# Second and third attention of a vision tower: score tiles of three heads over one image's own 37 keys, values spread by image, and a later fill of the routed rows

## The reference, cut to what matters

```python
# second: causal, B x 37 x 192, H = 12, D = 16
q, k, v = jnp.split(layer_norm(x, ln1_w) @ c_attn_w.T, 3, axis=-1)
scores = jnp.einsum('bhqd,bhkd->bhqk', q, k) * (1.0 / math.sqrt(D))
scores = jnp.where(causal, scores, -jnp.inf)
y = jnp.einsum('bhqk,bhkd->bhqd', softmax(scores), v)      # then @ c_proj_w.T, + x
# third: no token sees itself, one scale per head
attn = jnp.einsum('bhid,bhjd->bhij', q, k) * scale[None, :, None, None]
attn = jnp.where(diag[None, None, :, :], -jnp.inf, attn)
out = jnp.einsum('bhij,bhjd->bhid', softmax(attn), v)      # then @ w_proj.T + b_proj, + x
```

## Time and profile before

| what | value |
|---|---|
| median of 3 runs | 2166.01 us (2151.96 to 2166.42) |
| the profiled execution's own time | 2172.53 us |
| its span, first to last instruction | 2170.6 us |
| TensorE's mean granted clock | 0.817 of 2.4 GHz |
| TensorE busy | 1868.5 us, 86% |
| first attention and tokens | 0 to about 316 us |
| second attention, first mask to last projection | 316.0 to 484.4 us |
| ffn 0 and its routing | 484.4 to 640.7 us |
| third attention, first mask to last group before the fourth's projections | 648.3 to 820.4 us |
| all later stages | 848.4 to 2170.6 us |

### The profile page before, as it was taken

How to read it: one execution, slowest core, us unless ns; L and a number is a source line. 1 busy time by engine, 2 the same in 40 slices (tenths; PEclk the granted TensorE clock), 3 DMA queues, 4 the chain that set the end, 5 groups by cost and what they waited for, 6 DMA issues and landing times.

```text
span 2170.6 us, 35211 instructions
## 1 busy us (share of the span) xinstructions
PE 1868.5 (86%) x12440; PEld 1723.5 (79%) x12440; DVE 1134.4 (52%) x3189; ACT 799.2 (37%) x1907; POOL 588.7 (27%) x1369
## 2 busy tenths in 40 slices
PE   7999999996938997998999888977998999889980
PEld 7999888876937777988898778876888898788870
DVE  2423245554327554675577643345775577643436
ACT  1211124323414333553454334434454454334420
POOL 3333241231046433123422310025313412310021
PEclk8855557657966656998998899998999999799995
DMA  4039400003420000001000046651001000046630
GB/s 117 18 107 286 138 1 15 14 24 91 163 78 23 1 15 27 1 1 56 15 2 14 27 139 199 210 170 33 4 1 55 16 1 14 13 150 203 203 107 28
DMA packets 77409, 151.00 MB, mean 70 GB/s; under 512 B 6344, under 2 KB 56626, under 8 KB 77141
## 3 DMA queue, kind: packets, MB, share of 16 engines
q1 hardware_dynamic: 70902, 136.49, 19.7%
q0 software_dynamic: 6336, 12.26, 2.0%
HBM read 108.67 MB, written 41.05 MB: 69 GB/s over the span
## 4 chain that ended last, share of the span: by engine, by line
PE 52%; issue 16%; DVE 14%; DMA 6%; POOL 4%; SPq 3%; ACT 3%; another core or an unknown queue 0%; DVEq 0%; POOLq 0%; ACTq 0%
PE ps_proj L1020 9%; PE ps_o L1075 7%; PE ps_pt L994 6%; DMA w_in<-w_all_dram 5%; PE ps_proj L1095 5%; PE ps_score L1053 4%; PE ps_proj L1033 4%; PE ps_score L1166 4%; PE ps_proj L1149 3%; PE ps_proj L947 2%; SPq L823 2%; ACT w_hi L1281 1%; PE ps_score L968 1%; DVE prob L1439 1%; DVE negmax L1438 1%
## 5 line engine op out<-in xcount | busy, mean ns | idle before, releaser
L1166 PE MATMUL ps_score<-w,hid 128*112 128x192 f32 (+2 forms) x1680 | 306.3, 335 | 14.1 <-DVE x L1717 6.2
L1166 PEld LDWEIGHTS ps_score<-w,hid 128*112 128x112 f32 (+2 forms) x1680 | 278.0, 180 | 16.8 <-issue 8.5
L1330 POOL TENSOR_SCALAR tmp<-rs,var 111x1 f32<-111x1 f32 x154 | 55.4, 360 | 855.9 <-DVE rs L1410 855.4
L1260 ACT ACTIVATE probt<-ps_pt 111x333 f32<-111x333 f32 x308 | 137.8, 447 | 338.7 <-PE ps_pt L994 336.6
L994 PE MATMUL ps_pt<-const,prob 111*111 111x111 f32 x924 | 198.8, 335 | 52.6 <-ACT probt L1260 40.6
L1271 ACT ACTIVATE hid<-ps_proj 128x224 f32<-128x224 f32 (+2 forms) x360 | 133.6, 382 | 265.9 <-PE ps_proj L1149 252.4
L994 PEld LDWEIGHTS ps_pt<-const,prob 111*111 111x111 f32 x924 | 150.0, 223 | 89.7 <-issue 54.5
L1075 PEld LDWEIGHTS ps_o<-v,probt 111*111 111x111 f32 x1584 | 213.5, 215 | 1.1 <-issue 0.5
L1075 PE MATMUL ps_o<-v,probt 111*111 111x65 f32 (+1 forms) x1584 | 208.1, 282 | 0.0
L1318 POOL DMA_INDIRECT tin<-rows_out,idx x66 | 68.0, 1030 | 499.8 <-issue 384.0
L1255 ACT ACTIVATE prob<-prob 111x333 f32<-111x333 f32 x308 | 145.8, 477 | 62.9 <-DVE prob L1439 57.6
(11 more groups left out here) (239 smaller groups left out, 4381.0 us busy)
## 6 DMA issues: line engine op xcount, KB each, us to landing
w_in<-w_all_dram SPq DMA_DIRECT2D x66, 768.0 KB, 4.4
w<-w_all_dram SPq DMA_DIRECT2D x50, 576.0 KB, 5.2
rows_in<-w_lo SPq DMA_DIRECT2D x1, 12320.0 KB, 64.5
rows_out<-w_lo SPq DMA_DIRECT2D x1, 9240.0 KB, 90.1
tin<-rows_in SPq DMA_DIRECT2D x36, 224.0 KB
rows_out<-tout SPq DMA_DIRECT2D x36, 168.0 KB
patch<-patches_dram SPq DMA_DIRECT2D x11, 333.0 KB, 3.2
wo<-wo_all_dram SPq DMA_DIRECT2D x6, 576.0 KB, 3.8
```

What stands on the lines that cost most here:

```text
L1166: last = pe.matmul(bank[0:n, 0:C], hid[:, i % 2, m, at:at + n], w2[:, slot, m, :], start=(m == 0), stop=(m == FC - 1))
L1260: act.activation(probt[:, n % 4, :, :], ps_pt[0:TG, 0:3 * TG].rearrange("p (c n) -> p c n", c=3), ACT.Copy).then_inc(pt_taken, 1)
```

## The change

Q and K of the two attentions are laid out in 2 chunks instead of 3 each, so a block has 4 QK steps instead of 6. A chunk holds, at rows 0 to 47 and 64 to 111, three heads each. When ScalarE copies Q it does so three times, each time with a scale (hscale) that is zero but for one of the three heads; so for each image a tile of 111 columns arises: three heads by 37 queries. S multiplies it (stationary) by the 37 keys of the same image: 12 products of 111 by 37 per group instead of 12 of 111 by 111, in one unit of 4 x 111 columns over both PSUM banks, with two mask products of 222 columns instead of four of 333. VectorE takes one maximum and one subtraction over 444 columns, ScalarE one exponential, TensorE four transposes instead of twelve, ScalarE one copy.

V is copied three times by ScalarE with a scale that is 1 for the tokens of one image and 0 for the others, into vimg, where each head has three images' 16 values and one of ones each. PV is 12 products with 37 stationary columns (queries) and 51 moving ones (three images by 17), into 37 partitions. The output is turned by six transposes instead of two.

`short_order` is the new list: S(n), [slot 0], PV(n-1), E(n), [slot 1], PT(n), OT(n-1), [slot 2], Y(n-1), [slot 3]. There is one W1 step less in each of the two attentions: at the end of the first attention and at the end of ffn 0. The W1 of ffn 0's first matrix moves from g = 2 to n = 7 of CAUSAL; those of the T5 layer in DIAG from g = 2, 9, 10 to n = 2, 5 and 11. One more logit (8 for 7) and count (7 for 6) are computed within CAUSAL. The fill of rows_in and rows_out for ffn 2 is issued by SyncE at DIAG's second W1 (n = 5). `zero` is a tile of its own.

```diff
+        self.short = a in (CAUSAL, DIAG)
         self.d = T5_D if self.t5 else SMALL_D
         self.rows = 64 if self.t5 else 32
         self.per_chunk = 128 // self.rows
-        self.chunks = H // self.per_chunk
+        self.chunks = 2 if self.short else H // self.per_chunk
...
-        _n = 3 if ATTS[_st[1]].t5 else 2
+        _n = 3 if ATTS[_st[1]].t5 else 1
...
-        if n in (24, 32):
-            out.append(("W1", LOAD0[("att", CAUSAL)] + (n == 32)))
+        if n == 24:
+            out.append(("W1", LOAD0[("att", CAUSAL)]))
...
+COMB_SHORT = {0: ((3, 0), (4, 2)), 1: ((5, 0), (6, 2)), 2: ((7, 2),), 3: ((8, 2),), 4: ((9, 2),), 5: ((10, 2),)}
+LOGITS_AHEAD = {0: 8, 2: len(LOGIT_AT), 4: len(LOGIT_AT)}
+COUNTS_AHEAD = {0: 7, 2: len(COUNT_AT), 4: len(COUNT_AT)}
+def short_fill(a, n, last_stage, follower):
+    late = last_stage in COMBINED
+    slots = [[] for _ in range(4)]
+    if n < G:
+        b = BLOCK_OF[n]
+        i = n - BLOCKS[b][0]
+        if late:
+            for c, k in COMB_SHORT.get(n, ()):
+                slots[k].append(("prev", ("COMB", c)))
+                if c + GAT_RING < G:
+                    slots[k].append(("prev", ("GAT", c + GAT_RING)))
+        slots[0].append(("V", n, 0))
+        if b + 1 < NB:
+            g0, size = BLOCKS[b + 1]
+            places = [(0, 3), (1, 1), (1, 3)] if late else [(0, 1), (0, 3), (1, 1)]
+            for k, (at, slot) in enumerate(places[:size]):
+                if at == i:
+                    slots[slot].append(("A", g0 + k))
+            where = [(2, 0), (2, 1), (2, 2), (2, 3)] if late else [(1, 2), (1, 3), (2, 0), (2, 1)]
+            for j, (at, slot) in enumerate(where):
+                if at == i:
+                    slots[slot].append(("QK", b + 1, j))
+    if a == CAUSAL:
+        if 0 <= n - 3 < 9:
+            slots[2].append(("next", ("A", n - 3)))
+        if 0 <= n - 4 < LOGITS_AHEAD[0]:
+            slots[1].append(("next", ("L", n - 4)))
+        if 0 <= n - 5 < COUNTS_AHEAD[0]:
+            slots[3].append(("next", ("CNT", n - 5)))
+        if n == 7:
+            slots[3].append(("W1", LOAD0[follower]))
+    else:
+        if 2 <= n:
+            slots[3].append(("N2", n - 2))
+        if n in (8, 9, 10):
+            slots[2].append(("next", ("A", n - 8)))
+        if n in (2, 5):
+            slots[3].append(("W1", LOAD0[follower] + (n == 5)))
+        if n == G:
+            slots[0].append(("W1", LOAD0[follower] + 2))
+            first = [("next", x) for x in first_block(follower[1])]
+            slots[0] += first[:6]
+            slots[1] += first[6:12]
+            slots[3] += first[12:]
+    return slots
+def short_order(a, last_stage, follower):
+    out = first_block(a) if last_stage[0] == "ffn" else []
+    for n in range(G + 1):
+        slots = short_fill(a, n, last_stage, follower)
+        if n < G:
+            out.append(("S", n, 0))
+        out += slots[0]
+        if n:
+            out.append(("PV", n - 1, 1))
+        if n < G:
+            out.append(("E", n, 0))
+        out += slots[1]
+        if n < G:
+            out.append(("PT", n, 0))
+        if n:
+            out.append(("OT", n - 1, 0))
+        out += slots[2]
+        if n:
+            out.append(("Y", n - 1))
+        out += slots[3]
+    if a == DIAG:
+        out += [("N2", g) for g in range(G) if ("N2", g) not in out]
+    return out
...
-    if a == DIAG and g >= 3:
-        slots[5].append(("N2", g - 3))
...
-    out = [("L", 7), ("A", 8), ("CNT", 6), ("L", 8), ("A", 9), ("CNT", 7), ("L", 9), ("CNT", 8), ("A", 10),
-           ("CNT", 9), ("L", 10), ("CNT", 10), ("GATE",), ("X", 0)]
+    out = [("L", 8), ("A", 9), ("CNT", 7), ("L", 9), ("CNT", 8), ("A", 10), ("CNT", 9), ("L", 10), ("CNT", 10),
+           ("GATE",), ("X", 0)]
...
-            if k == E - 1 and m in (2, 4):
-                out.append(("W1", LOAD0[("att", DIAG)] + m // 4))
+            if k == E - 1 and m == 2:
+                out.append(("W1", LOAD0[("att", DIAG)]))
...
-            n = DISPATCH[2].units * DISPATCH[2].width // TL
-            sp.dma_start(rows_in[2].rearrange("k r n -> (k r) n").rearrange("(p t) n -> p t n", p=TL),
-                         zero.unsqueeze(1).to_broadcast([TL, n, CX])).then_inc(rows_zero, 16)
-            n = DISPATCH[2].units * DISPATCH[2].width // TL
-            sp.dma_start(rows_out[2].rearrange("k r n -> (k r) n").rearrange("(p t) n -> p t n", p=TL),
-                         zero[:, 0:C].unsqueeze(1).to_broadcast([TL, n, C])).then_inc(rows_zero, 16)
+            def later_fill():
+                n = DISPATCH[2].units * DISPATCH[2].width // TL
+                sp.dma_start(rows_in[2].rearrange("k r n -> (k r) n").rearrange("(p t) n -> p t n", p=TL),
+                             zero[:].unsqueeze(1).to_broadcast([TL, n, CX])).then_inc(later_zero, 16)
+                sp.dma_start(rows_out[2].rearrange("k r n -> (k r) n").rearrange("(p t) n -> p t n", p=TL),
+                             zero[:, 0:C].unsqueeze(1).to_broadcast([TL, n, C])).then_inc(later_zero, 16)
             for st, step in PROGRAM:
                 kind = step[0]
                 if kind == "W1":
                     next_load(step[1] + 1)
+                    if step[1] == LOAD0[("att", T5)] + 1:
+                        later_fill()
...
-                for i in range(3):
-                    last = pe.transpose(ps_pt[0:TG, i * TG:(i + 1) * TG], prob[:, n % 4, i, :], ident)
+                for i in range(4 if ATTS[a].short else 3):
+                    src = short_ring(prob, n)[:, i * TG:(i + 1) * TG] if ATTS[a].short else prob[:, n % 4, i, :]
+                    last = pe.transpose(ps_pt[0:TG, i * TG:(i + 1) * TG], src, ident)
...
+                    if s.short:
+                        if SCORE[(*key, 0)] % 2:
+                            banks.reverse()
                         for bank in banks:
-                            pe.matmul(bank[0:TG, 0:3 * TG], identb[:], maskb[:, a, :, :].rearrange("p h k -> p (h k)"),
+                            pe.matmul(bank[0:TG, 0:2 * TG], identb[:],
+                                      maskb[:, a, 0:2, :].rearrange("p h k -> p (h k)"),
                                       start=True, stop=False, skip_group_check=True)
+                        for j in range(2):
+                            for i in range(IPG):
+                                for e, bank in enumerate(banks):
+                                    at, col = 64 * e, (j * IPG + i) * NTOK
+                                    ins = pe.matmul(bank[0:TG, col:col + NTOK],
+                                                    short_q(b % 2)[at:at + 64, j, g - BLOCKS[b][0], i, :],
+                                                    short_k(b % 2)[at:at + 64, j, t0 + i * NTOK:t0 + (i + 1) * NTOK],
+                                                    start=False, stop=True, skip_group_check=True)
+                                    if (j, i) == (1, IPG - 1):
+                                        ins.then_inc(score_full, 1)
+                        return
...
+                    if s.short:
+                        turned_p = short_ring(probt, unit(a, g, 0))
+                        wide = IPG * (SMALL_D + 1)
+                        for h in range(H):
+                            at = (h // 3 % 2 * 2 + h // 6) * TG + h % 3 * NTOK
+                            col = h % 6 * wide
+                            last = pe.matmul(ps_o[0:NTOK, h // 6, col:col + wide], turned_p[:, at:at + NTOK],
+                                             vimg[:, g % 2, h * wide:(h + 1) * wide], start=True, stop=True,
+                                             skip_group_check=True)
+                        last.then_inc(o_full, 1)
+                        return
...
+                    if s.short:
+                        for c, n in ((0, 128), (1, 64)):
+                            for i in range(IPG):
+                                at = c * TG + i * NTOK
+                                last = pe.transpose(bank[0:n, at:at + NTOK],
+                                                    o[0:NTOK, g % 2, i * C + c * 128:i * C + c * 128 + n],
+                                                    ident[0:NTOK, 0:NTOK])
...
+                    if a >= T5:
+                        act.activation(qk[:, b % 2, j, 0:n], bank[:, 0:n], ACT.Copy).then_inc(taken, 1)
+                    elif j >= 2:
+                        act.activation(short_k(b % 2)[:, j - 2, 0:n], bank[:, 0:n], ACT.Copy).then_inc(taken, 1)
+                    else:
+                        src = bank[:, 0:n].rearrange("p (g t) -> p g t", t=TP)[:, :, 0:TG] \
+                            .rearrange("p g (i q) -> p g i q", i=IPG)
+                        for h in range(3):
+                            ins = act.activation(short_q(b % 2)[:, j, 0:BLOCKS[b][1], :, h * NTOK:(h + 1) * NTOK], src,
+                                                 ACT.Copy, scale=hscale[:, a - CAUSAL, j, h:h + 1])
```

(38 more changed lines are left out.)

147 lines of the change are left out of this document (84 added, 63 removed).

## The result

Over the runs shown, the kernel after takes 1998.3 us (median of 4, 1992.6 to 2001.1), the kernel before beside it 2159.0 (2133.3 to 2166.4): a ratio of 0.932, 95% interval 0.924 to 0.940. The profiled executions are 1996.2 and 2172.5 us, a gain of 176 us where 107 were forecast; by the medians it is 161 us. The time is outside the range, on the fast side.

What follows compares the result with a forecast made beforehand. TensorE's instruction stream and clock were taken as the bound; gains of 45 (second attention), 45.5 (third) and 16 us elsewhere made 107, from 2172.5 to 2065.5, or 2059 from the median; forecast 2035 to 2080, outer range 2014 to 2104.

Steps and rivals of the forecast that it cites:

- This W1 is gone: 4.3 us: First attention: removing the W1 step whose read was queued behind the zeros saves TensorE's wait, 4.3 us.
- Steady shares: Second and third attention: the share of time at 2.4 GHz stays as before, granted clock near 0.65.
- Rival C: Second and third attention: the clock rises to a share of 0.7, stages 106 and 104 us, whole 2019; chance 0.12.
- Scores: Second and third attention: 24 pairs a group at 100 ns, 2.4 us at 1.2 GHz (was 2.78); 1.54 at 2.4.
- Values: Second and third attention: 24 pairs a group at 104 ns, 2.5 us at 1.2 GHz (was 4.22); 1.6 at 2.4.
- OT: Output transposes per group: 576 stationary columns at 1.6 ns, 1.05 us with its end; 0.55 at 2.4 GHz.
- PT's: Wait for shift and exponential ahead of PT: covered at 1.2 GHz, 0.1 us open a group at 2.4 GHz.
- The zeros: Moved to the third attention at no cost, landing about 165 us after its start; wo's margin 10 to 15 us.
- B: Rival: the clock stays at 1.2 GHz in second and third attention, 70 us gained, 2096 us; chance 0.13.
- D: Rival: score and value pairs get no cheaper, 116 and 176 ns, 2097 us; chance 0.07.
- E: Rival: the moved zeros hold up wo of the fourth attention by 10 to 15 us, 2071 us; chance 0.03.
- F: Rival: slower, exposed softmax handovers; 2176 us, decided at 3.3 us added idle time per group; chance 0.03.

Runs made afterwards that it cites:

- b_again: The kernel before, unchanged, profiled once more: 2153.2 us in the profiled run, first attention 291.9 us.
- q1: The kernel before with each mask product of the first attention issued twice from the second group on: 2135.2 us, ratio 0.994.
- e2: The kernel after with the zeros moved back under the first attention, all else as changed: 2011.5 us, ratio to before 0.923.
- n1: k2 with each mask product of the first attention issued twice from the second group on: 1967.4 us, ratio to before 0.916.
- k2: The kernel after with two idle products ahead of each OT and three ahead of each Y, second attention alone: 1968.2 us, ratio to before 0.920.
- m1: n1 with three idle products ahead of each OT and four ahead of each Y in the second attention: 1966.9 us, ratio to before 0.916.
- a_ref: The kernel after, unchanged, as the reference for kernels timed beside it: 1985.1 us, ratio to before 0.925.
- n1_repeat: n1 unchanged, run again as the reference for m1: 1972.3 us, ratio to before 0.920.

## Why the prediction was right or wrong

**Where it failed.** The term "This W1 is gone: 4.3 us" was mis-sized: TensorE's idle time at the low clock was read as the price of the late read, and at 2.4 GHz that read costs 47 us. In the first attention the change gained 72.4 us: 24.1 are the clock's other course (316.0 to 291.9 us, one program), and 47.0 the read behind the zeros (291.9 to 244.9, both at 2.4 GHz from 100 to 181 us; 45.3 in e1, which moves the zeros alone; 1.3 lie between the two profiles of the kernel after). In the kernel before each hides the other: the low clock hid the wait, and the wait hides most of the high clock, which b_again and q1 show. So the low clock costs the kernel before 24 us, the kernel after some 60 (305.4 to 243.6 and 244.9). Which course a run takes was luck, and the profile of before had the slow one: without it the gain of 176 would have been about 24 smaller, and still above the forecast. The rows for it were there: ScalarE idle for 17.5 us, a read of 44.6 us, and TensorE at 0.5 there. What was not asked is where TensorE would have been at the other clock, the one that every other stage shows in part.

**The clock elsewhere.** Steady shares were forecast, 0.66 and 0.62; 0.66 and 0.68 came. Rival C's sign was right for the kernel as a whole, but its place was wrong: the clock rose in the stage that no rival looked at, and there to a course that the unchanged kernel takes too.

**The products.** Scores: forecast 2.4 us, measured 2.39; at 2.4 GHz 1.54, measured 1.29, since 64 ns was only the shortest spacing of the old kernel. Values: 2.5 and 1.6, measured 2.19 and 1.23. PT 1.03, measured 0.93. OT 1.05, measured 0.65: 1.13 ns for each of 576 stationary columns and not 1.6; no run shows why. V was put at 0.91 and took 1.18 us. Y is 1.55 to 1.87, as taken (1.70). The sum of these steps and the masks (0.37) is 9.4 us where 9.96 were forecast; but whole groups from mask to mask at 1.2 GHz took 15.1 to 15.7 us before and 11.4 to 12.3 after, 3.5 saved and not 4.6, as turns and logits add to them. At 2.4 GHz one and the same group of the second attention took 10.8 before and 7.9 after, 2.9 saved and not 2.2. The two errors nearly cancel, so that 41.0 and 47.6 us came for 45 and 45.5 is in part luck.

**The waits.** Y's wait is 0.6 us at most, as forecast, and OT's 0 to 1.0 (0.25 and 0.5). PT's was put at 0.1 us; three of them made 6.9 us, the longest behind a W1 step whose VectorE half stands ahead of the shift. That step was not followed.

**The zeros.** Moved at no cost, right: the third attention takes 114.4 us from first to last mask with them (after) and without (e2). They landed 49.5 and 83.1 us after their issue, the second at some 686 us, 160 us after the stage's start (165 forecast). wo was issued at 682.4 us behind them and first used at 700.1, and no wait for it stands in the profile.

```profile
rows_in<-zero SPq DMA_DIRECT2D x1, 12320.0 KB, 49.5
rows_out<-zero SPq DMA_DIRECT2D x1, 9240.0 KB, 83.1
```

**Rivals.** B and D fell by the clock and the pair times; E by the same wo; F by waits of 1.2 us a group in the mean (6.9 + 3.4 + 2.8 over the 11 groups of the third attention), not 3.3, though single ones reached 3.0.

## What to carry to other kernels

A stage ends at the later of its arithmetic and its transfers; when a wait looks small, work out where the engine would stand at the other clock before calling the transfer cheap, and look at everything queued ahead of it. Where a kernel is bound by TensorE with narrow products, a few dense idle products in its waits can pay for themselves; one has to try it by stage and look at the stages behind it too, since in n1 the next one took 13 us more. The best versions here (k2, n1, m1) lie at 1967 to 1974 us, k2 12.7 us under the kernel after on the same chip (mean of six runs 1969.1, of five of a_ref's six 1981.9; its sixth took 2048.1).

## What the runs showed of the hardware

- TensorE's clock takes two courses in one program: at 1.2 GHz from 109 us on, or at 2.4 GHz to 181, with no difference in the instructions. In n1, n1_repeat, q1 and m1, with more dense columns, all four profiles had the high course and no dip from 36 to 176 us; without them 12 of 16 had it, each with a dip between 60 and 96 us. So the dip is shown to go, but not that the low course can't come.
- A busy TensorE does not always get the high clock: in the kernel before it was busy for 93.0 of 93 us from 107 us on, at 0.51.
- Within one row group a pair of load and product takes about the longer of the two: 91 ns at 1.2 GHz with 37 stationary and 51 moving columns, 125 with 74 and 51 (117 by this reading), 162 to 176 with 111 and up to 37. Row groups in turn put two loads side by side (100 ns).
- A pair of 37 or 51 moving columns takes 51 to 54 ns at 2.4 GHz.
